# Shared weights laid out ahead, gate exponentials inside a tile, and three pairs of result buffers, in an attention and mixture-of-experts kernel

## The reference

```python
x = x + xattn(layernorm(x), k, bias, ctx, ctx, 8)
x = x + moe(layernorm(x), gate_w, gate_up_proj, down_proj, shared_gate_w, shared_up_w, shared_down_w)

# xattn: per head i and j of 8, causal convolution along the 512 columns
kv = vr[:, :, :, None, :] * x2r[:, :, None, :, :]
y = conv(kv, k) + kv * skip
out = einsum('bhijl,bhil->bhjl', y, x1r)

# moe: 64 experts, 6 of them for each token
scores = softmax(xf @ gate_w.T); topk_w, topk_idx = top_k(scores, 6)
# each expert: a list of at most 128 tokens, hidden width 192
hid = silu(g) * u;  eo = (hid @ down_proj) * weight;  routed += eo at its tokens
# shared expert for all tokens, hidden width 384
shared = (silu(xf @ shared_gate_w.T) * (xf @ shared_up_w.T)) @ shared_down_w.T
return routed + shared
```

## Time and profile before

| | us |
|---|---|
| median of 3 runs (1158.91 to 1162.35) | 1161.11 |
| the profiled execution, in full | 1163.35 |
| its span, first to last instruction | 1161.5 |
| PE busy | 1086.0 (94%) |
| DVE busy | 828.7 (71%) |
| POOL busy | 736.9 (63%) |
| ACT busy | 527.3 (45%) |
| HBM traffic | 187 GB/s over the span |

### The profile page before, as it was taken

The page is one execution under the profiler, slowest core; times in us unless marked ns, Lnnn a source line. Parts: engine busy times, 40 slices in busy tenths (PEclk is TensorE's granted clock), DMA queues, the critical chain, the costliest instruction groups (busy, mean ns, idle before and its releaser), DMA issues. The chain is left out here.

```text
span 1161.5 us, 17623 instructions
## 1 busy us (share of the span) xinstructions
PE 1086.0 (94%) x5113; PEld 851.7 (73%) x5113; DVE 828.7 (71%) x1424; ACT 527.3 (45%) x958; POOL 736.9 (63%) x434
## 2 busy tenths in 40 slices
PE   3999999999999999999699999999999799999953
PEld 2778777787777777877599998777777567777632
DVE  3799999999999999998589963555655345655623
ACT  5565556555665556553422222444434334444411
POOL 6999999999999999993024223245345245445422
PEclk9999999999999999999899999999999889999977
DMA  6365554456445554452385445699999889999964
GB/s 188 97 189 159 165 146 135 146 158 166 129 135 157 165 148 134 144 151 73 109 269 154 129 127 153 197 286 284 294 289 280 222 255 289 291 280 282 284 166 52
DMA packets 92029, 217.08 MB, mean 187 GB/s; under 512 B 11239, under 2 KB 16167, under 8 KB 91856
## 3 DMA queue, kind: packets, MB, share of 16 engines
q1 hardware_dynamic: 75440, 177.75, 50.5%
q0 software_dynamic: 16544, 38.78, 15.8%
HBM read 164.82 MB, written 52.18 MB: 187 GB/s over the span
## 5 line engine op out<-in xcount | busy, mean ns | idle before, releaser
L1059 POOL TENSOR_TENSOR ring<-vT,pT 128x1024 f32<-128x1024 f32 x128 | 249.2, 1958 | 9.5 <-ACT vT L803 9.3
L445 PE MATMUL Y<-split,toep 128*128 128x512 f32 x576 | 238.2, 414 | 11.1 <-ACT toep L797 8.9
L1067 POOL TENSOR_TENSOR split<-ring,split 128x1024 fp32r<-128x1024 f32 x96 | 231.0, 2406 | 1.1 <-ACT split L809 1.1
L447 PE MATMUL Y<-split,toep 128*128 128x512 f32 x576 | 227.2, 394 | 0.0
L446 PE MATMUL Y<-split,toep 128*128 128x512 f32 x576 | 225.9, 392 | 0.0
L689 PE MATMUL Y<-ring,xT 128*128 128x384 f32 x512 | 194.3, 503 | 0.0
L1236 DVE TENSOR_TENSOR z<-Y,cT 128x1024 f32<-128x1024 f32 x128 | 157.0, 1226 | 26.6 <-PE Y L449 25.5
L1242 DVE TENSOR_REDUCE o<-z 128x128 f32<-128x1152 f32 x128 | 172.1, 1345 | 1.2
L445 PEld LDWEIGHTS Y<-split,toep 128*128 128x128 f32 x576 | 109.0, 189 | 31.2 <-issue 9.8
L809 ACT ACTIVATE split<-ring 128x1024 fp32r<-128x1024 f32 x96 | 100.8, 1050 | 58.2 <-POOL ring L1059 58.2
L447 PEld LDWEIGHTS Y<-split,toep 128*128 128x128 f32 x576 | 108.6, 189 | 24.4
(11 more groups left out here) (168 smaller groups left out, 1909.7 us busy)
## 6 DMA issues: line engine op xcount, KB each, us to landing
ring<-_L_ffn_gate_up_proj_dram SPq DMA_DIRECT2D x64, 768.0 KB
ring<-in_L_ffn_down_proj_dram SPq DMA_DIRECT2D x64, 384.0 KB
gr<-filters SPq DMA_DIRECT2D x32, 512.0 KB, 4.1
stage<-in_x_dram SPq DMA_DIRECT2D x32, 256.0 KB, 5.5
pT<-in_turned_dram SPq DMA_DIRECT2D x32, 256.0 KB, 4.1
cT<-in_turned_dram SPq DMA_DIRECT2D x32, 256.0 KB, 4.1
xr<-in_x_dram SPq DMA_DIRECT2D x32, 256.0 KB, 3.9
xn_rows<-xn SPq DMA_DIRECT2D x32, 256.0 KB, 2.9
```

Source lines behind the costliest of these rows:

```text
L445: pe.matmul(y, high, kv[:, s, 0, a, n], start=(a == 0), stop=False)
L447: last = pe.matmul(y, low, kv[:, s, 0, a, n], start=False, stop=(a == c))
L1059: pool.tensor_tensor(to.rearrange("p (b j i) -> p b j i", i=NH, j=NH), a, d, ALU.mult).then_inc(kvp_ready, 1)
L1067: pool.tensor_tensor(kv[:, s, 1, c, :], kvp[c], kv[:, s, 0, c, :].bitcast(F32), ALU.subtract).then_inc(kv_ready, 1)
```

## The change

- **Laid-out shared weights.** The three weights come in already turned, as one array `shared_rows` made from the inputs, one row of 6 KB per partition. There are no `turn_weights`. ScalarE copies each whole weight (128 x 1536) to the high part inside the last attention tile, from SBUF; GpSimd makes the low parts of gate and up after its last attention tile, DVE that of down. The first two tiles of the shared stage are loaded into `pT` instead of `xn`, and so earlier. The order at the seam is written anew on all engines.
- **Exponentials at tile 8.** ScalarE takes one exponential of all of `sc_all` between its tiles 8 and 9.
- **Sums in a tile without search.** DVE sums and scales in tile GATE_AT = 10, which has no round of the search; the rounds run in t = 2 to 9 and 11 to 18. The scaled scores are written out in t = 13 to 20.
- **Three pairs of result buffers.** `eo` has NO = 3 pairs (the third is `pT`); a copy waits for the additions of three pairs before, not two.
- **Groups of 3, 3, 2, 2.** Shared tiles are added at pairs 6, 15, 21 and 27.
- **Gathers further ahead.** A pair's two gathers are issued two experts further ahead, and always before `add_shared`.
- **Start.** x is loaded before k; the first context tile, the skip terms and the first filter load are issued earlier; ScalarE begins with a square root, whose table is so loaded first.

```diff
+GATE_AT = 10
-BATCH = 5
+GROUPS = (3, 6, 8, 10)
+NO = 3
...
         eo = [[y[:, 0, :], y[:, 1, :]], [w[:, 0, :], w[:, 1, :]],
+              [pT[:, n, :, :].rearrange("p c n -> p (c n)") for n in range(2)]]
+        PL = [TA, DX]
...
+            load_rows(0, 0)
             sp.dma_start(kin, k).then_inc(k_in, 16)
-            load_rows(0, 0)
...
             load_rows(1, 1)
+            sp.wait_ge(filters_out, 48)
+            load_filter(0)
             load_paired(1, 1)
...
+            for t in range(2):
+                b_load_xT(t, t)
             store_xT(NT - 2, 0)
+            b_load_xT(2, 0)
+            sp.wait_ge(z_done, NC * NT)
+            sp.wait_ge(o_done, NC * NT)
+            sp.dma_start(place, c_order).then_inc(order_in, 16)
             store(NT - 1, 1, late=True)
...
 # TensorE after the attention loop
+            pe.wait_ge(z_done, NC * NT - 1)
+            pe.wait_ge(b_xT_lo, 1)
+            pe.wait_ge(sh_lo, 1)
+            b_half(0, 0, 0)
             turn_o(NT - 1, 1)
+            pe.wait_ge(sh_lo, 2)
+            b_half(0, 0, 1)
+            pe.wait_ge(z_done, NC * NT)
+            pe.wait_ge(b_xT_lo, 2)
+            b_half(1, 1, 0)
             pe.wait_ge(xT_sb, NT - 1)
             turn_xn(NT - 1, 1)
+            b_half(1, 1, 1)
             pe.wait_ge(sc_ready, NT - 1)
             router(NT - 1, 1)
+            b_turn_hid(0, 0)
+            pe.wait_ge(b_xT_lo, 3)
+            pe.wait_ge(b_hid, 1)
+            b_half(2, 0, 0)
             places(0)
             places(1)
+            pe.wait_ge(x1_ready, NT)
+            pe.wait_ge(sh_d_lo, 1)
+            b_out(0, 0)
+            b_turn_hid(1, 1)
+            b_half(2, 0, 1)
             places(2)
             places(3)
+            pe.wait_ge(place_sb, 4)
+            b_out(1, 1)
...
 # ScalarE
+            act.wait_ge(dve_setup, 2)
+            act.activation(sd2[:], eps[:], ACT.Sqrt)
             act.wait_ge(k_in, 16)
...
+            with act.Fori(0, 3) as i:
+                b_iteration(i * 2 + 3, 1)
+                b_iteration(i * 2 + 4, 0)
+            act.wait_ge(sc_kept, NT)
+            act.activation(sc_all[:], sc_all[:], ACT.Exp).then_inc(exp_ready, 1)
+            with act.Fori(3, NB // 2 - 2) as i:
...
 # GpSimd
+            for n in range(2):
+                pool.wait_ge(sh_hi, n + 1)
+                pool.tensor_tensor(shared_to[n][1], shared_from(n), shared_to[n][0].bitcast(F32),
+                                   ALU.subtract).then_inc(sh_lo, 1)
...
             for k in range(E // 2):
+                for e in range(2 * k + NG if k else NG - 2, min(2 * k + NG + 2, E)):
+                    fetch(e)
                 t, part = pieces(2 * k + 1)
+                if part == "out" and t - NB + 1 in GROUPS:
                     add_shared(t, k)
                 for a in range(2):
                     add(k, a)
...
 # DVE after the attention loop
             times(NT - 1, 1, 3)
+            b_rows_low(0, 0)
             best_logit(NT - 2)
             total(NT - 1, 1, 3)
             scores(NT - 2)
+            b_rows_low(1, 1)
             add_x1(NT - 1, 1)
             stats2(NT - 1, 1)
             mean2(NT - 1)
+            best_scores(NT - 2)
+            six_scores(NT - 2)
             rstd2(NT - 1)
             shift2(NT - 1)
             experts_marked(NT - 2)
+            shared_down_low()
+            b_hidden(0, 0)
             best_logit(NT - 1)
             scores(NT - 1)
             best_scores(NT - 1)
             six_scores(NT - 1)
             experts_marked(NT - 1)
+            b_rows_low(2, 0)
+            b_hidden(1, 1)
+            b_hidden_low(0, 0)
             order_places(0)
             order_places(1)
+            b_result(0, 0)
             order_places(2)
             order_places(3)
...
-                if k < 2:
+                if k < NO:
                     dve.wait_ge(y_out[1], NB // 2 * 16)
                 else:
-                    dve.wait_ge(added[1], (k - 1) * 16)
-                dve.tensor_copy(eo[k % 2][1], DN[1][:, :]).then_inc(eb_ready, 1)
+                    dve.wait_ge(added[1], (k + 1 - NO) * 16)
+                dve.tensor_copy(eo[k % NO][1], DN[1][:, :]).then_inc(eb_ready, 1)
```

More of the change, by code:

```diff
@@ L225, in weights, with shared_from, b_rows @@
                          down[e].rearrange("(p c) n -> p (c n)", p=IH)).then_inc(weights_in[r], 16)
[L228 to L236, removed]
+        shared = [ring[:, n, 0:n_up * L] for n in range(3)]
+        shared_to = [[sh_gu[:, a, :, g * SI:(g + 1) * SI] for a in range(2)] for g in range(2)]
+        shared_to.append([sh_d[:, a, :, :] for a in range(2)])
+        def shared_from(n):
+            return shared[n].rearrange("p (c i) -> p c i", c=n_up if n == 2 else NC)
+        def b_rows(t, s):
+            return pT[:, s, :, :].rearrange("p c n -> p (c n)") if among(t, 0, 1) else xn[:, s, :]
         def pieces(e):
@@ L469, in router @@
                 last.then_inc(logit_ps, 1)
[L471 to L493, removed]
             def iteration(h, s):
@@ L556, in places @@
                     m = g * 4 + n
-                    last = pe.matmul(DN[g % 2][:, n * P:(n + 1) * P], mask[:, 2 * m:2 * m + 2, :], ident16[:],
+                    last = pe.matmul(PL[g % 2][:, n * P:(n + 1) * P], mask[:, 2 * m:2 * m + 2, :], ident16[:],
                                      start=True, stop=True)
@@ L1110, in shared_done @@
             def shared_done(k):
-                return sum(pieces(2 * n + 1)[1] == "out" for n in range(k + 1)) // BATCH * BATCH
+                done = sum(pieces(2 * n + 1)[1] == "out" for n in range(k + 1))
+                return max((g for g in GROUPS if g <= done), default=0)
             def add(k, a):
@@ L1158, in add_shared @@
                     pool.wait_ge(added[a], k * 16)
-                for t in range(last + 1 - BATCH, last + 1):
+                for t in range(NB + shared_done(k - 1), last + 1):
                     pool.wait_ge(y2_ready, t - NB + 1)
@@ L1487, in b_iteration @@
                 b_result(t - 1, 1 - s)
-            for n in range(NF):
-                b_iteration(n + 2, n % 2, n)
-            for t in range(MOVE_AT, NB):
-                b_iteration(t, t % 2)
+            for t in range(2, NB):
+                n = t - 2 - (t > GATE_AT)
+                b_iteration(t, t % 2, n if t != GATE_AT and n < NF else None)
                 if t == MOVE_AT + 2:
@@ L1625, in turned, with shared_rows @@
     return ctx.reshape(B, NT, NH, NC, P).transpose(1, 4, 3, 0, 2).reshape(NT, P, L)
+def shared_rows(gate, up, down):
+    up_parts = [a.reshape(SI, P, NC).transpose(1, 2, 0).reshape(P, NC * SI) for a in (gate, up)]
+    down_part = down.T.reshape(SI // P, P, L).transpose(1, 0, 2).reshape(P, SI // P * L)
+    return np.stack(up_parts + [down_part])
 def kernel(**inputs):
@@ L1637 @@
     data.append(("turned", turned(_np.asarray(inputs["ctx_2048"]))))
+    shared = [_np.asarray(inputs[f"L0_ffn_shared_{n}_w"]) for n in ("gate", "up", "down")]
+    data.append(("shared_rows", shared_rows(*shared)))
     for name, value in data:
```

208 lines of the change are left out of this document (63 added, 145 removed).

## The result

The changed kernel takes 1150.79 us (median of 9 runs, 1146.31 to 1154.42); the kernel before took 1160.22 beside it (9 runs, 1152.08 to 1162.35). The ratio is 0.9938, 95% interval 0.9919 to 0.9956: 9.4 us by the medians, 7 by the ratio (5 to 9). Forecast were 19.9 us, to 1141. The time lies inside the stated range, outside the forecast's own (1134 to 1149), and nearest to rival E (1151), though not for E's reason: in the profiled execution the expert stage gained nearly what was forecast, and the shared stage gave most of the seam's gain back.

The account below looks back on a forecast made before the run. TensorE, with GpSimd nearly equal, was taken to bound attention, and TensorE with DMA a later stretch. Terms 1.8 + 9.2 - 0.6 + 9.5 = 19.9 us gave 1143.4, 1141 at the median; own range 1134 to 1149, stated range 1128 to 1156.

Parts of the forecast that it names:

- rival E: Expert stage is pinned by DMA and gives nothing; 10.4 us gained in all, total 1151; chance 0.10.
- Exponentials at tile 8: Shared stage: exponential with two table loads after ScalarE tile 8, sums at tile 10; 0.6 us lost (0 to 2.5).
- The start: Before the first convolution: overlapped table load and a vanished GpSimd wait, less later k; 1.8 us gained (0.5 to 2.9).
- The seam: Attention to shared stage: tile 3 starts 11.2 us earlier, less 2 for the clock; 9.2 gained (5 to 11.2).
- three waits in the places named: Seam: TensorE waits 1.3, 2.8 and 3.8 us for low parts of rows, tile 2's rows and hidden 1.
- The expert stage: Pairs of experts and their output additions: shorter tail and a third buffer pair keeping DMA fed; 9.5 us gained.
- Its two terms: Expert stage: four group waits of 49.6 us together, and 11.6 us for each expert pair's two additions (a link).
- the step from the length of the chain to the end: Expert stage: chain of additions gains 3.9 us and the tail 3.0, taken as 6.9 off the end.
- The base: Whole kernel: profiled execution of 1163.35 us lies 2.2 above the median 1161.11, so 1143.4 becomes 1141.
- B: Expert stage: chain of additions runs at 12.3 us per pair of experts; 1.9 us gained in all, 1159; chance 0.12.
- D: Expert stage: additions take 13.25 us per pair of experts; 29 us lost there, total 1180; chance 0.06.
- C: Expert stage: third buffer pair absorbs every delay; 20 us gained there, 30 in all, total 1131; chance 0.22.

Follow-up runs that it names:

- x1: Changed kernel with ScalarE's tiles 9 and 10 of the shared stage written out after the exponential, ahead of the loop: 1144.85 us, ratio to before 0.9880.
- x5: Kernel before with one tiny square root directly ahead of ScalarE's loop over the shared tiles: 1168.02 us, ratio 1.0077.
- x10: x7 with the old start on SP and ScalarE (k first, old load places, no square root ahead): 1139.29 us, ratio 0.9839.
- x7: x6 with DVE making the low part of hidden 1 ahead of the first maximum instead of behind it: 1138.56 us, ratio 0.9828.
- x3: Changed kernel with two pairs of result buffers instead of three: 1157.20 us, ratio 0.9975.
- x4: Kernel before with only the third pair of result buffers added: 1157.53 us, ratio 0.9988.
- x8: x1 with the gathers in their old place, not two experts further ahead and behind a group when there is one: 1150.98 us, ratio 0.9946.
- x2: Changed kernel with the old two groups of five shared tiles, three buffer pairs kept: 1148.46 us, ratio 0.9908.
- x6: x1 with two groups of five shared tiles: 1141.48 us, ratio 0.9852.
- x9: x7 with k loaded ahead of x again: 1138.63 us, ratio 0.9827.

## Why the prediction was right or wrong

**The failed step is "Exponentials at tile 8".** It priced the block of two loads and one exponential at 0.6 us, once. The block itself is as described (1.28, then the exponential 0.01 us later). What was missed is that the exponential was put between two loops, and so the second loop is entered with another table than its own end leaves; the loads then stand inside the loop, in all six passes. 12 loads of 1.28 us late in a chain from ScalarE over DVE to TensorE cost 7.3 of the 7.6 us by the profile and 6 by the medians (x1), and the same mechanism, alone in the kernel before with 18 loads, 9 (x5). The 0.3 that are left in x1 are the block itself and the sums at tile 10, for which 0.6 had been taken. The upper end given for this step, 2.5, was too low as well: the diff showed `Exp` directly ahead of a second `Fori`, and the question of what each pass must then load was not asked. With 7.6 in place of 0.6 the same sum is 12.9 and the forecast 1148; the rest of the miss is below.

**The start: 1.8 forecast, 1.0 in the profile.** The mean of x came 0.82 us later, not 0.6, and moved GpSimd's first product by only 0.25 where 1.28 - 0.6 = 0.7 had been worked out; and this execution has the new wait of 0.44. Over seven executions with this start the average lies 1.6 ahead of x10 with the old one, so the term is right in size. Its parts are not: the product gives 0.25, the wait that goes the rest (1.14 in the kernel before, 1.53 in x10). That they add up to the forecast is luck.

**The seam: 9.2 forecast, 8.8.** Right, by its own steps: three waits in the places named, within 0.4 us each, and the clock in between full and half. Over the executions start and seam together gave 9.5 (tile 3 at 577.9 on average of the six kernels with this seam, 577.17 to 578.91; at 587.4 of the three with the old one), of 11.0 forecast. x7 shows that the last wait, put down to the maximum standing ahead of the low part, was named rightly.

**The expert stage: 9.5 forecast, 8.8 in the profile, 7.2 by the medians.** Its two terms came as forecast, 50.5 against 49.6 for the groups and 11.46 against 11.6 a link, and the hole was filled. x3, x4 and x8 support the reason given (slack of a third pair, gathers ahead of the groups), and add that neither gives much without the other. What did not hold is the step from the length of the chain to the end, on which 6.9 of the 9.5 stand. In x2 the chain is 5.9 us shorter than in the changed kernel and the whole 2 to 3.5; with two groups of five TensorE is busy for 349.22 of the 350 us from 740 to 1090, with the small groups for 343.98, with 4.21 us of wait for gathered rows at 961.21, behind the second group. So the small groups themselves rather cost 2 to 3 us (x2 and x6), and that 9.5 was met so closely is in part luck.

**The base.** The profiled execution, 1163.35, was taken to lie 2.2 above the median. Beside the changed kernel and the experiments the kernel before has medians of 1160.22, 1158.5, 1158.64 and 1158.07, so it lay 3 to 5 above. The profiled gain was 11.0, the medians' 9.4: the difference, 1.6, is one of base and belongs to no step.

Of the rivals, B and D (links at 12.3 and 13.25) are refuted by 11.46; and C (20 us) and E (none) by the 8.8 gained in that stage (5 to 7 by the runs). The Trainium skill (ScalarE: Activation LUTs, What ACT_TABLE_LOAD costs) adds a drain of about 1380 ns to each switch of tables, by which this step was estimated at 2 us lost. The drain does not show in this case: the load at 614.13 ends at 615.41 and the exponential starts at 615.42, and the copy at 646.72 ends at 647.35 with the next load at 647.37. The error lay in the count of loads, not in the price of one.

## What to carry to other kernels

Count ScalarE's table loads per loop pass and not per function: wherever a function of another table stands directly ahead of a loop, write the first pass out (x1; to move the function elsewhere was not tried), and look in the trace for loads that repeat. When two resources guard one stage (here result buffers and gathers), removing one wait hands the time to the other; change them together and read which wait is left. A gain made ahead of a seam is kept only as far as the seam's clock and its waits allow, so read each gain at a wait that is common to both kernels rather than at the end, and in several executions: at equal code such a wait lay up to 0.9 us apart here.

## What the runs showed of the hardware

- A loop whose entry and whose end leave different tables had two loads of 1.28 us in each pass, one of them before a copy which, written in line behind the exponential, needed none (x1).
- TensorE's granted clock in the seam differs from execution to execution at equal code: the pass of twelve near 560 us took 2.36 (x7), 3.43 (changed kernel) and 4.21 us (x9). From the first wait to tile 3 x7 takes 25.4 us and x9, with equal code there, 28.3; that hides edits of 1 us at the start.
- A shorter wait of TensorE kept the clock for the pass behind it: 3.27 to 4.18 us behind a wait of 4.14 (six kernels), 2.31 or 2.32 behind one of 1.71 (three).
- The next link starts 10.3 to 15.7 us after a group of two or three shared tiles (DMA share 1.04 and 1.05 behind the first three groups, 0.81 behind the last). The numbers don't grow evenly with the group: 12.85 and 15.70 for the same three tiles. In x3 it is the other way round, 14.60 and 12.90, so the place of the group alone does not set it; what does was not tried.
